# Window attention, fp16 halves: V as the stationary operand in four column groups, transposed attention output, denominators by a ones matmul, bias through the projection

## The reference

```
xn  = group_norm(x)                        # no scale, no shift
qkv = windows(xn) @ qkv_w + qkv_b          # 512 windows of 77 tokens, 192 -> 576
attn = softmax(q @ k.T / sqrt(24))         # per window and head, 77 x 77
out = (attn @ v) @ proj_w + proj_b         # 192 -> 192
y = x + unwindow(out)
```

## Time and profile before

| | |
|---|---|
| time, two runs | 2107.02 and 2124.22 us, median 2115.62 |
| profiled execution | 2107.97 us |
| its span, first to last instruction | 2105.9 us |
| mean granted TensorE clock | 0.937 |
| busy: PE, DVE, ACT, POOL | 1691.6, 1515.2, 1299.1, 1608.9 us |
| chain that ended last, by engine | PE 58%, DVE 26%, issue 10%, DMA 3% |

### The profile page before, as it was taken

The page is one execution under the profiler, slowest core; times in us unless marked ns, Lnnn a source line. Parts: engine busy times, 40 slices in busy tenths (PEclk is TensorE's granted clock), DMA queues, the critical chain, the costliest instruction groups (busy, mean ns, idle before and its releaser), DMA issues.

```text
span 2105.9 us, 97027 instructions
## 1 busy us (share of the span) xinstructions
PE 1691.6 (80%) x41742; PEld 1500.7 (71%) x41742; DVE 1515.2 (72%) x3672; ACT 1299.1 (62%) x2659; POOL 1608.9 (76%) x2060
## 2 busy tenths in 40 slices
PE   0003899988898888988898989988898889988886
PEld 0002788877787778877787878777787778887775
DVE  6772677777677776777777777777777777777783
ACT  0002667767676676766676766766676666767763
POOL 0004689888888898888888998988888888988864
PEclk9999899999999998999999998999999999999996
DMA  6881101111111111111111111111111111111110
GB/s 159 226 232 39 45 20 51 46 57 40 38 57 57 56 57 57 42 54 40 41 54 57 57 57 57 57 39 57 39 50 46 57 57 57 57 48 48 39 39 38
DMA packets 17134, 127.74 MB, mean 61 GB/s; under 512 B 1921, under 2 KB 2178, under 8 KB 2434
## 3 DMA queue, kind: packets, MB, share of 16 engines
q1 hardware_dynamic: 16770, 121.91, 17.1%
HBM read 91.62 MB, written 30.28 MB: 58 GB/s over the span
## 4 chain that ended last, share of the span: by engine, by line
PE 58%; DVE 26%; issue 10%; DMA 3%; ACT 1%; POOL 1%; DVEq 1%; SPq 0%; ACTq 0%; POOLq 0%
PE ps_a L676 25%; PE ps_q L676 8%; PE ps_q L775 6%; PE ps_k L676 6%; PE ps_s L715 6%; DVE v_lo L587 5%; DVE v_hi L641 5%; DVE q_lo L588 5%; DMA x_stat<-in_x 3%; PE ps_b L761 3%; DVE y_blk L627 2%; PE ps_b L676 2%; DVE q_hi L634 2%; DVE k_lo L588 2%; DVE stat L541 2%
## 5 line engine op out<-in xcount | busy, mean ns | idle before, releaser
L343 POOL TENSOR_TENSOR p_lo<-probs,p_hi 77x1232 f16<-77x1232 f32 x256 | 646.8, 2526 | 220.2 <-ACT p_hi L404 217.0
L434 ACT ACTIVATE probs<-ps_s,exp_shift,exp_scale 77x1232 f32<-77x1232 f32 x256 | 351.8, 1374 | 258.1 <-PE ps_s L715 246.1
L676 PE MATMUL ps_a<-v_hi,p_hi 77*128 77x25 f16 x4096 | 362.8, 174 | 84.6 <-DVE v_lo L587 81.9
L676 PEld LDWEIGHTS ps_a<-v_hi,p_hi 77*128 77x128 f16 x4096 | 330.1, 97 | 124.4 <-issue 122.0
L588 DVE SCALAR_TENSOR_TENSOR q_lo<-ps_q,b_qk,q_hi 128x154 f16<-128x154 f32 x512 | 170.4, 376 | 327.9 <-PE ps_q L775 327.9
L596 DVE TENSOR_REDUCE neg_max<-ps_s 77x16 fp32r<-77x1232 f32 x256 | 365.8, 1429 | 34.5 <-PE ps_s L730 34.5
L676 PE MATMUL ps_a<-v_hi,p_lo 77*128 77x25 f16 x4096 | 361.6, 174 | 0.0
L676 PE MATMUL ps_a<-v_lo,p_hi 77*128 77x25 f16 x4096 | 361.2, 174 | 0.0
L676 PEld LDWEIGHTS ps_a<-v_lo,p_hi 77*128 77x128 f16 x4096 | 323.3, 97 | 0.0
L676 PEld LDWEIGHTS ps_a<-v_hi,p_lo 77*128 77x128 f16 x4096 | 321.8, 97 | 0.0
L404 ACT ACTIVATE p_hi<-probs 77x1232 f16<-77x1232 f32 x256 | 310.0, 1211 | 0.3
(11 more groups left out here) (147 smaller groups left out, 5693.5 us busy)
## 6 DMA issues: line engine op xcount, KB each, us to landing
x_stat<-in_x SPq DMA_DIRECT2D x16, 1848.0 KB, 9.9
x_norm<-in_x SPq DMA_DIRECT2D x32, 924.0 KB
y_blk<-in_x SPq DMA_DIRECT2D x32, 924.0 KB
out<-y_blk SPq DMA_DIRECT2D x32, 924.0 KB
wA<-in_qkv_w SPq DMA_DIRECT2D x1, 288.0 KB
wB<-in_qkv_w SPq DMA_DIRECT2D x2, 144.0 KB
pA<-in_proj_w SPq DMA_DIRECT2D x1, 96.0 KB
pB<-in_proj_w SPq DMA_DIRECT2D x2, 48.0 KB
```

Source lines behind the costliest of these rows:

```text
L343: nc.gpsimd.tensor_tensor(p_lo[(s - 1) % 2][:, 0:16 * TOK], probs[:, :], p_hi[(s - 1) % 2][:, 0:16 * TOK], ALU.subtract).then_inc(pool_p, 1)
L434: nc.scalar.activation(probs[:, :].rearrange("p (g a n) -> p g a n", g=NG, a=4), scores(), ACT.Exp, bias=exp_shift[0:TOK, :], scale=exp_sc ...
L676: last = mm(dst, lhsT, rhs, start=first and n == 0, stop=closes and n == len(pairs) - 1, skip_group_check=True)
```

## The change

- **Attention output.** V becomes the stationary operand (77 x 32 columns: 24 channels, a one, seven zeros) and the probabilities move, 77 columns. The four heads of a group go to the four column groups of the array and so to partitions 0, 32, 64 and 96 of `ps_a`; the output has channels on partitions and tokens along the row, already transposed. Three passes, each over the four heads.
- **Denominators.** A matmul with a stationary block of ones (77 x 32) sums the probabilities over tokens and repeats the sum on all 32 partitions of a head: 16 matmuls a slot of 154 columns into `ps_b` (new function `denominators`).
- **Normalising.** DVE takes the reciprocal of all 128 x 308 denominators and multiplies; both stand first in its slot, with `O_LAG` 3. `oT_hi` is one ACT copy, `oT_lo` one POOL subtraction. `o_sb`, `o_split` and their transposes go.
- **Projection.** Its weights get the same layout with gaps (two halves of 128 rows, `p32`), so a tile takes 6 matmuls instead of 5. The rows with the ones carry the output bias, as two fp16 halves that DMA writes into `wp_hi`; the bias addition of POOL goes. `P_LAG` becomes 12.
- **Orders.** V is made for pair `i` and not `i+1`; its high half moves from DVE to ACT. On PE projection and V stand right behind the row scores, then K, the max matmuls, half of the attention output, transposed scores, Q, the other half, denominators, transposes of `x` (now into `ps_k`).

The core of the diff:

```diff
-P_LAG = PAIRS + O_LAG
+P_LAG = PAIRS + O_LAG + 1
...
+        ones16 = sb("ones16", [TOK, ROW_G], F16)
...
+        den_inv = sb("den_inv", [128, NUM])
+        o32 = [sb(f"o32_{p}", [128, NUM]) for p in range(2)]
...
+            sp.wait_ge(setup_w, 2)
+            sp.dma_start(wp_hi[HD:HD + 1, 0, :], bias_hi[:, :]).then_inc(dma_bias, 16)
+            sp.dma_start(wp_hi[ROW_G + HD:ROW_G + HD + 1, 0, :], bias_lo[:, :]).then_inc(dma_bias, 16)
...
+                    nc.gpsimd.tensor_tensor(oT_tokens(oT_lo, o), by_column(o32[o % 2]), oT_tokens(oT_hi, o),
+                                            ALU.subtract).then_inc(pool_oT, 1)
...
-                    nc.gpsimd.tensor_tensor(y, y, bias, ALU.add).then_inc(pool_y, 1)
...
+                    nc.scalar.activation(oT_tokens(oT_hi, o), by_column(o32[o % 2]), ACT.Copy).then_inc(act_oT, 1)
...
+                    reach(act, pe_v, i + 1)
+                    nc.scalar.activation(v_hi[s % V_BUFS][:, :, 0:HD],
+                                         ps_a[0:TOK, 0:2 * CH].rearrange("p (h d) -> p h d", d=HD), ACT.Copy)\
+                        .then_inc(act_v, 1)
...
+                if exists(i - O_LAG):
+
+                    reach(dve, pe_av, i - O_LAG + 1)
+                    reach(dve, act_oT, i - O_LAG - 1)
+                    reach(dve, pool_oT, i - O_LAG - 1)
+                    nc.vector.reciprocal(den_inv[:, :], ps_b[:, 0:NUM]).then_inc(dve_recip, 1)
+                    reach(dve, dve_recip, i - O_LAG + 1)
+                    tt(o32[(s - O_LAG) % 2][:, :], ps_a[:, 0:NUM], den_inv[:, :], ALU.mult).then_inc(dve_norm, 1)
                 if exists(i):
 
                     reach(dve, pe_scores, i + 1)
...
-                    nc.vector.reciprocal(recip[:, :, :], av[:, :, HD:HD + 1]).then_inc(dve_recip, 1)
...
-                    nc.vector.tensor_copy(v_hi[v_now][:, :, 0:HD], v_psum).then_inc(dve_v_hi, 1)
...
+                    for n, (v, p) in enumerate(((v_hi[v_now], p_hi[p_now]), (v_lo[v_now], p_hi[p_now]),
+                                                (v_hi[v_now], p_lo[p_now]))):
+                        for o, h, g, at in outs:
+                            last = mm(o, v[:, h, :], p[:, g, at:at + TOK], start=n == 0, stop=n == 2,
+                                      skip_group_check=True)
+                return last
+
+            def denominators(s):
+
+                for w in range(2):
+                    for n, p in enumerate((p_hi[s % 2], p_lo[s % 2])):
+                        for g in range(NG):
+                            d = ps_b[ROW_G * g:ROW_G * (g + 1), 0:NUM].rearrange("p (a w r) -> p a w r", w=2, r=WIN_H)
+                            last = mm(d[:, :, w, :], ones16[:, :], p[:, g, 2 * w * TOK:2 * (w + 1) * TOK],
+                                      start=n == 0, stop=n == 1, skip_group_check=True)
                 return last
...
+                if exists(i - P_LAG):
+
+                    if exists(i - O_LAG):
+                        reach(pe, dve_recip, i - O_LAG + 1)
...
+                        for j in range(NJ):
+                            passes += [(hi[:, j, t0 + c, :], wp_hi[:, j, :]), (hi[:, j, t0 + c, :], wp_lo[:, j, :]),
+                                       (lo[:, j, t0 + c, :], wp_hi[:, j, :])]
+                        last = products(ps_b[0:PART, c * CH:(c + 1) * CH], passes)
+                    last.then_inc(pe_proj, 1)
+                if exists(i):
...
+                    reach(pe, dve_norm, i - O_LAG + 1)
+                    buf, pair = parity(s), s % PAIRS
...
-                if exists(i - T_LAG):
...
+                    reach(pe, pool_p, i - AV_LAG + 1)
+                    if exists(i):
+                        reach(pe, dve_v, i + 1)
...
+                    denominators(s - AV_LAG).then_inc(pe_av, 1)
```

More of the change, by code:

```diff
@@ L70 @@
 PAD = FULL - TOK
+NUM = 4 * TOK
+BIAS_ROOM = 1024.0
 AUG_ONE = 32768.0
@@ L122, in window_attention @@
         xT = [sb(f"xT{p}", [128, 3, COLS + PAD], F16) for p in range(2)]
-        oT = [sb(f"oT{p}", [128, 3, TILES, PART], F16) for p in range(2)]
+        oT_hi = [sb(f"oT_hi{p}", [128, NJ, TILES, PART], F16) for p in range(2)]
+        oT_lo = [sb(f"oT_lo{p}", [128, NJ, TILES, PART], F16) for p in range(2)]
         def sb_qk(name):
@@ L130, in window_attention @@
         k_lo = [sb_qk(f"k_lo{p}") for p in range(2)]
-        v_hi = [sb(f"v_hi{p}", [TOK, 2 * HEADS, HD + 1], F16) for p in range(V_BUFS)]
-        v_lo = [sb(f"v_lo{p}", [TOK, 2 * HEADS, HD + 1], F16) for p in range(V_BUFS)]
+        v_hi = [sb(f"v_hi{p}", [TOK, 2 * HEADS, ROW_G], F16) for p in range(V_BUFS)]
+        v_lo = [sb(f"v_lo{p}", [TOK, 2 * HEADS, ROW_G], F16) for p in range(V_BUFS)]
         neg_max = sb("neg_max", [TOK, 4, NG, ROW_G], F32R)
[L135 to L140, removed]
+        ones16 = sb("ones16", [TOK, ROW_G], F16)
+        probs = sb("probs", [TOK, NG, 4 * TOK])
+        p_hi = [sb(f"p_hi{p}", [TOK, NG, 4 * TOK], F16) for p in range(2)]
+        p_lo = [sb(f"p_lo{p}", [TOK, NG, 4 * TOK], F16) for p in range(2)]
+        den_inv = sb("den_inv", [128, NUM])
+        o32 = [sb(f"o32_{p}", [128, NUM]) for p in range(2)]
         ps_s = ctx.enter_context(nc.psum_tensor("ps_s", [128, NG, 512], F32))
@@ L433, in slot @@
                     reach(act, pool_p, i)
[L434 removed]
+                    nc.scalar.activation(probs[:, :, :].rearrange("p g (a n) -> p g a n", a=4), scores(),
                                          ACT.Exp, bias=exp_shift[0:TOK, :], scale=exp_scale[0:TOK, :])\
                         .then_inc(act_exp, 1)
[L437 to L443 removed]
             slots(act, slot)
@@ L603, in slot @@
                     last.then_inc(dve_q, 1)
+                if exists(i):
+                    reach(dve, act_v, i + 1)
+                    lo_part(v_lo[s % V_BUFS][:, :, 0:HD], ps_a[0:TOK, 0:2 * CH].rearrange("p (h d) -> p h d", d=HD),
+                            v_hi[s % V_BUFS][:, :, 0:HD]).then_inc(dve_v, 1)
                 if exists(i + 1):
@@ L652, in _ @@
             pe.wait_ge(setup_w, 1)
-            mm(ps_a[0:PART, 0:CH], bvA_rep[:, :], pA[:, :], start=True, stop=False)
-            mm(ps_a[0:PART, 0:CH], bvB_rep[:, :], pB[0:CB, :], start=False, stop=False)
-            mm(ps_a[0:PART, 0:CH], ones[0:1, :], b_proj[:, :], start=False, stop=True).then_inc(pe_bias, 1)
+            for j in range(NJ):
+                mm(ps_a[:, 0:CH], bv_rep[:, j, :], p32[:, j, :], start=j == 0, stop=False)
+            mm(ps_a[:, 0:CH], ones[0:1, :], b_proj[:, :], start=False, stop=True).then_inc(pe_bias, 1)
             mean_v = stat6[:, :, :, :, :].rearrange("p b h g (e t) -> p (b h g) e t", e=2)[:, :, :, 1]
```

279 lines of the change are left out of this document (122 added, 157 removed).

## The result

The changed kernel takes 3214.2 us (two runs, 3212.12 and 3216.3) against 2115.62: a ratio of 1.520, 95% interval 1.505 to 1.536. The forecast was 3020 us, slower, in the range 2440 to 3440. The direction, the mechanism and the range hold; the size is 194 us short.

A forecast was written before the change was run, and what follows sets the result against it. Before: PE and DVE pass work to and fro, PE carrying most of the loop. Forecast: 255 slots of 10.78 us (2749), 267 outside and 2 between span and execution, say 3020 us, range 2440 to 3440.

The forecast's parts named there:

- The reciprocal: DVE, head of each slot: 128x308 reciprocal takes 2.08 us, priced at 6.29 ns a column, and PE's projection waits for it.
- The holes: PE stands still twice a slot: some 1.8 us under the reciprocal, some 1.4 us from max matmuls to the end of `v_lo`.
- The column groups: PE: four column groups run beside each other, half the attention output 0.27 us (0.45 half clock); rival, not shared, 2945 us, 8%.
- loads of 32 columns: PE: by the skill's rule column tiling switches off fast weight load, estimated 27 ns a load, a slot about 0.9 us longer.
- The half-clock slot: One slot's loop at 1.2 GHz sums to 12.44 us; as a rival, half clock throughout, 3440 us, 10%.
- The clock: PE's clock goes to and fro, a third of the time at full clock, giving 10.78 us a slot; chance 66%.
- The attention output ahead of the transposed scores: PE: its first half waits for `v_lo`; `q_lo` and `v_lo` 1.14, signal 0.05, half the attention output 0.27 us at full clock.
- DVE the busiest engine: Sign of a right forecast: over the whole run DVE would be busier than any other engine.
- Outside the slots, and the loop's end: Start and end 209.4 + 39.9 us, set-up and drain together 3 more, and 15 us for 15 loop-body ends.
- Full clock throughout, 2440: Rival: every slot at 2.4 GHz, 8.51 us each, total 2440 us; chance 12%.
- Not slower: Rival: the long reciprocal costs 0.5 us like an ordinary pass, slot 6.93 us, 2036 us if the clock holds; chance 4%.
- The gain and the row of PE: PE: array work falls a net 0.6 us a slot; before, PE's row was nearly unbroken, one 0.33 us hole for `q_lo`.

The follow-up runs named there:

- the filled kernel: Changed kernel plus 11 useless matmuls a slot on PE, 6 ahead of the row scores and 5 behind the max matmuls: 2580.0 us, clock 0.976.
- The kernel with the pass: Changed kernel with an ordinary DVE pass (product with 1e-6) in place of the long reciprocal, output not normalised: 2526.9 us, clock 0.803.
- the reordered kernel: Kernel before, with the second half of K and the transposes of `o_split` ahead of the attention output on PE: 2059.2 us, ratio 0.977.
- changed, filled, attention output moved: Changed kernel, first half of attention output moved behind Q, 9 useless matmuls a slot (6 ahead of row scores, 3 behind max matmuls): 2403.3 us.
- changed, ordinary pass, attention output moved: Changed kernel, first half of attention output behind Q, ordinary DVE pass for the reciprocal (output not normalised), no useless matmuls: 2047.8 us.
- The move: Changed kernel with the first half of the attention output moved on PE from ahead of the transposed scores to behind Q; alone 2770.5 us, clock 0.801.

## Why the prediction was right, and where it was short

- **The reciprocal: right.** 2083 ns against 2.08 us. Two column counts of one operation in the trace gave the price of a third. Doubling it, and adding it alone to the kernel before, moved the slot by 1.94 and 1.93 us, so it lies on the path as forecast. Its two bounds, 0.5 and 2.11 us, were 400 us apart over the slots; the row of the same operation was the one to trust.
- **The holes: right at full clock, the first one too long at half.** The second is 1.31 us (forecast 1.4). The first, 2.13 less the row scores in the forecast, is 1.70 at full clock (1.8); at half clock it is 1.14, because the transposes of `x`, which the forecast left out of it, run under the reciprocal too.
- **The column groups: right.** Second half of the attention output 0.42 us at half clock (0.45), denominators 0.58 (2172.44 to about 2173.02 by 0.145 a group; forecast 0.52). The 0.9 us a slot that the prediction worked out for loads of 32 columns did not come.
- **The half-clock slot: 0.4 us short.** The forecast of 12.44 has 1.32 us for the mean of 1.375 tiles; with the one tile of the slot shown (0.96) it is 12.08, and 12.48 was measured. By the rows: first half of the attention output 0.56 instead of 0.45; `q_lo` to attention output 1.27 instead of 1.19; from Q to the reciprocal 2.68 instead of 2.49. These are mostly gaps where blocks of different shape meet (last section), which my start-to-start sums inside one block left out. At full clock the loop is 8.76 us for 1.375 tiles (8.57 and 9.07), 0.25 over the 8.51. The gaps are over half of the miss.
- **The clock: the step that failed.** "I take a third of the time at full clock." The mean clock over the slots was 0.63, which is 26% of the time at 2.4 GHz. With my own two slot lengths that is 0.26/8.51 + 0.74/12.44 = 0.0900 slots a us, 11.11 us each; with both longer by the 0.4 above it is 11.52, and with the loop's ends 11.58, where 11.57 was measured. So the two terms are the miss, the clock's share 0.33 and the gaps 0.41 us a slot. The third was a guess that no row gave. That it would go to and fro was right; of the 255 slots, 64 were at half clock throughout and one at full. The idle time in the earlier trace rows, 0.56 of 3.38 us, does not decide it alone: the filled kernel stands 1.5 us in the slot shown, at 1.00.
- **The attention output ahead of the transposed scores: right on the path, missed as a cause.** Its 1.14 + 0.05 + 0.27 stood in the sum. But I put the clock down to both holes alike and gave this one no price of its own. The runs give it one: 177 us at a high clock, 444 us with the clock free to answer.
- **"DVE the busiest engine": wrong.** DVE has 57%, PE 71%, since at half clock PE's instructions are longer.
- **Outside the slots, and the loop's end: nearly right.** 264 us against 252: the set-up is 7 us longer instead of 0 to 3, and the drain another 7. The loop-end stall of PE (2.68 us) lies mostly over the reciprocal: the `neg_max` behind it was 1.04 us late, forecast 1.
- **Full clock throughout, 2440: out as a case of this kernel,** but the filled kernel is close to it, at 2580.
- **"Not slower", a reciprocal priced like an ordinary pass: its price was wrong too.** It had 6.93 us a slot and 2036 us "if the clock holds". The kernel with the pass took 2526.9: the clock did not hold, and its slots at full clock take 7.21 and 7.46 us (one tile, two), since PE's transposes and row scores take the place of the pass on the path.
- **The gain and the row of PE: small errors.** The forecast's net 0.6 us a slot on the array is 0.5 by its own terms (0.68 + 0.20 - 0.28 - 0.11). And PE's row before has not one hole of 0.33 us but two: the second is the wait of the attention output for `v_lo`, shown at the reordered kernel.

Slots that were at full clock throughout can be compared without the clock (medians in us, from `neg_max` to `neg_max`):

| kernel | one tile | two tiles |
|---|---|---|
| before | 6.79 | 6.80 |
| changed, filled | 8.57 | 9.07 |
| changed, filled, attention output moved | 7.91 | 8.40 |
| changed, ordinary pass | 7.21 | 7.46 |
| changed, ordinary pass, attention output moved | 6.55 | 6.80 |

The move takes off 0.66 us with the reciprocal and with the pass alike, and the pass 1.36 to 1.6 us with the move and without: on the path the two causes add up. The changed kernel itself gives such a slot only once.

Put together, as a chain of kernels that each differ by one step: filling the holes 3214 to 2580, the clock, 634 us; moving the attention output 2580 to 2403, its wait on the path, 177 us; the ordinary pass (and no more fill, which cost nothing there) 2403 to 2048, the length of the reciprocal, 355 us; and 2048 is 60 us under the kernel before, which is what the layout saves. The steps would come out otherwise in another order, since the clock answers to the other two, and each is good to some tens of us. The runs show after which stretches the clock fell or rose, and no more; which of the two fills matters more was not tried, nor was the changed kernel with the reciprocal behind `neg_max`.

## What to carry to other kernels

Broadcasting denominators over partitions turned a reciprocal of 16 columns into one of 308: read the price per column of that very operation from the trace before moving it to a wide shape, and ask what stands behind it in every engine's queue. Where two engines pass work round a ring, price each hole twice, once as time and once as clock: here a move worth 0.66 us a slot on the path, some 170 us in all, brought 444 us, and useless matmuls in two holes brought 634. Test a layout with its suspected cost taken out; it shows whether the idea is bad or only one operation of it.

## What was not expected of the hardware

- With PE standing 1.1 and 1.3 us in slots of 12.5 us (1.7 and 1.3 at full clock) the mean clock was 0.65. With one hole of 0.76 us and a short reciprocal, in slots of 6.3 to 6.8 us, it was 0.95, and with two of 0.89 and 0.63 us, in slots of 8.6 to 9.1, 0.98.
- Each change on PE between the full array, row groups and column groups costs about 0.1 us beyond the matmuls, at either clock: six groups of the attention output by 0.072 make 0.43 at half clock, and 0.56 passed until the transposed scores (2169.15 to 2169.71), while the second half, followed by another block in column groups, took 0.42. The same 0.1 us stands between the transposed scores and Q, Q and the attention output, and the denominators and the transposes, and between row groups and the full array in the kernel before too. Why was not tried.
- A stationary operand of 32 columns costs nothing that could be seen: four matmuls of 77 columns take 0.04 us on four column groups and 0.16 on one at full clock, 0.07 and 0.29 at half.
